# A fused neighbourhood-attention block on one core: VectorE's instruction list reordered within the band loop

## The reference

```python
h1 = n1_w * arcsinh(h) + n1_b
q, k, v = split(h1 @ qkv_w + qkv_b)            # 8 heads of 32
scores = q * hd**-0.5 . k[3 x 3 neighbourhood] # clipped at the image's edge
out = softmax(scores) @ v[3 x 3 neighbourhood]
h = h + out @ proj_w + proj_b
h2 = n2_w * arcsinh(h) + n2_b
return h + gelu(h2 @ mlp_w1 + mlp_b1) @ mlp_w2 + mlp_b2
```

## Time and profile before

| | |
|---|---|
| median of three runs | 4443.3 us |
| the profiled execution | 4440.94 us |
| its span, first to last instruction | 4439.1 us |
| mean granted TensorE clock | 0.992 of full speed |
| busy PE / DVE / ACT / POOL | 94% / 88% / 82% / 76% |

### The profile page before, as it was taken

The page is one execution under the profiler, slowest core; times in us unless marked ns, Lnnn a source line. Parts: engine busy times, 40 slices in busy tenths (PEclk is TensorE's granted clock), DMA queues, the critical chain, the costliest instruction groups (busy, mean ns, idle before and its releaser), DMA issues.

```text
span 4439.1 us, 129514 instructions
## 1 busy us (share of the span) xinstructions
PE 4159.5 (94%) x49224; PEld 2857.8 (64%) x49224; DVE 3926.1 (88%) x8225; ACT 3631.7 (82%) x5377; POOL 3359.0 (76%) x4092
## 2 busy tenths in 40 slices
PE   5999999999999999999999999999999999999997
PEld 3666666666666666666666666666666666666664
DVE  6899999989989998998999899899989989999984
ACT  4888888888888888888888888888888888888884
POOL 2777777777777777777777777777777777777775
PEclk8999999999999999999999999999999999999998
DMA  4555555555555555555555555555555555555551
GB/s 120 132 141 139 142 139 143 136 139 141 141 140 140 142 137 139 141 140 141 140 142 137 140 141 139 140 141 141 139 139 144 136 140 140 141 141 138 142 133 50
DMA packets 644105, 607.94 MB, mean 137 GB/s; under 512 B 77070, under 2 KB 639376, under 8 KB 639888
## 3 DMA queue, kind: packets, MB, share of 16 engines
q1 hardware_dynamic: 643488, 599.66, 51.2%
HBM read 206.02 MB, written 135.40 MB: 77 GB/s over the span
## 4 chain that ended last, share of the span: by engine, by line
DVE 42%; PE 18%; POOL 13%; issue 13%; ACT 12%; SPq 1%; DMA 0%; POOLq 0%; DVEq 0%; ACTq 0%
PE ps L381 16%; POOL b_lo L1163 6%; POOL b_hi L1161 6%; DVE ps L841 5%; DVE queries L860 5%; DVE o_norm L874 4%; DVE ln_u L767 4%; DVE ln_u L760 4%; DVE k_nat L815 4%; ACT L1073 4%; DVE ln_u L763 3%; DVE h L802 3%; ACT p_hi L1064 3%; DVE q_nat L808 3%; ACT prob L1063 2%
## 5 line engine op out<-in xcount | busy, mean ns | idle before, releaser
L1146 POOL TENSOR_TENSOR p_lo<-prob,p_hi 100x512 f16<-100x512 f32 x1024 | 1269.7, 1245 | 619.1 <-ACT p_hi L1064 619.1
L1063 ACT ACTIVATE prob<-ps 100x512 f32<-100x512 f32 x1024 | 610.2, 596 | 51.1 <-PE ps L381 49.3
L874 DVE TENSOR_TENSOR o_norm<-ps,recip 64x128 f32<-64x128 f32 x2048 | 590.2, 288 | 49.3
L1172 POOL TENSOR_TENSOR g_lo<-g,g_hi 128x512 f16<-128x512 f32 x512 | 593.8, 1160 | 41.0
L1064 ACT ACTIVATE p_hi<-ps 100x512 f16<-100x512 f32 x1024 | 616.4, 602 | 0.0
L381 PEld LDWEIGHTS ps<-v_win,p_hi 100*128 100x128 f16 x8192 | 476.0, 98 | 204.7 <-issue 66.9
L381 PE MATMUL ps<-w_hi,g_hi 128*128 128x256 f16 x2048 | 561.1, 274 | 0.0
L841 DVE TENSOR_REDUCE ps<-ps 128x8 f32<-128x800 f32 x512 | 509.1, 994 | 58.6 <-PE ps L381 54.2
L381 PE MATMUL ps<-w_lo,g_hi 128*128 128x256 f16 x2048 | 560.9, 274 | 0.0
L381 PE MATMUL ps<-w_hi,g_lo 128*128 128x256 f16 x2048 | 560.8, 274 | 0.0
L381 PE MATMUL ps<-v_win,p_hi 100*128 100x65 f16 x8192 | 515.6, 193 | 27.0 <-POOL p_lo L1146 18.4
(11 more groups left out here) (100 smaller groups left out, 11497.9 us busy)
## 6 DMA issues: line engine op xcount, KB each, us to landing
keys<-k_win SPq DMA_DIRECT2D x1536, 100.0 KB, 2.3
v_win<-v_rows SPq DMA_DIRECT2D x1024, 101.6 KB
queries<-q_nat SPq DMA_DIRECT2D x1536, 64.0 KB
v_rows<-v_nat SPq DMA_DIRECT2D x256, 260.0 KB, 4.3
xin<-in_x_dram SPq DMA_DIRECT2D x128, 512.0 KB, 4.3
out_dram<-y SPq DMA_DIRECT2D x256, 256.0 KB, 3.0
queries<-in_query_mask_dram SPq DMA_DIRECT2D x128, 224.0 KB
keys<-in_mlp_w_dram SPq DMA_DIRECT2D x2, 512.0 KB, 6.5
```

The costliest lines, as they stand in the source:

```text
L874: s = v.tensor_tensor(o_norm[r, c], av[r, :, HD * e:HD * e + HD], recip[c % 2][r].to_broadcast([NQ, PAIRS, HD]), ALU.mult)
L1063: act.activation(prob[b][0:NK], ps[0:NK, B_ST + b, :], ACT.Exp, scale=INV * INV).then_inc(prob_ready, 1)
L1146: pool.tensor_tensor(p_lo[b][0:NK], prob[b][0:NK], p_hi[b][0:NK], ALU.subtract).then_inc(p_lo_ready, 1)
L1172: pool.tensor_tensor(g_lo[:, m, :], g32[:, m, :], g_hi[:, m, :], ALU.subtract).then_inc(g_lo_ready, 1)
```

## The change

The change moves calls in two lists; no instruction is added or taken away. On DVE, within the slots:

- slot 0: `k_low` 1 goes in front of the copies `maxima_to_queries`;
- slot 1: `q_low` 1 and x's first evacuation go in front of the copies; x's second evacuation stays behind them;
- slot 2: `sign2` goes in front of `maximum`, and `sum1_` in front of the copies;
- slot 3: `sign1` and then `o_low` (first half) go in front of `maximum`.

On PE, in slot 3 only, `max_rows` goes from in front of `mlp_in` 2 to behind it, in front of `mlp_in` 3. In slots 0 to 2 it stays where it was.

```diff
                     if att:
                         weighted(t, par, 2 * k)
-                    if more:
+                    if k < 3 and more:
                         max_rows(ahead[0], ahead[2])
...
                     if k == 3 and post:
                         mlp_in(t - 1, 2)
+                    if k == 3 and more:
+                        max_rows(ahead[0], ahead[2])
+                    if k == 3 and post:
                         mlp_in(t - 1, 3)
...
                 for k in range(SLOTS):
                     ta, ka = (t, k + 1) if k + 1 < SLOTS else (t + 1, 0)
                     more = has(ta)
+                    if k == 2 and post:
+                        sign2(t - 1, old)
+                    if k == 3 and fill:
+                        sign1(t + 3, (u + 3) % XT)
+                    if k == 3 and att:
+                        o_low(t, par, 0)
                     if more:
                         maximum(ta, ka)
                         maximum_high(ta, ka)
...
                     if k == 1 and pre:
                         q_low(t + 2, par, 0)
-                    if k == 2 and post:
-                        sign2(t - 1, old)
-                    if k == 3 and att:
-                        o_low(t, par, 0)
-                    if k == 3 and fill:
-                        sign1(t + 3, (u + 3) % XT)
 
                     if att:
                         sum_reciprocal(t, 2 * k)
                         normalise(t, 2 * k)
-                    if more:
-                        maxima_to_queries(ta, par if ta == t else old, ka)
-
                     if k == 0 and pre:
                         k_low(t + 2, 1)
-                    if k == 0 and post:
-                        h_from_projection(t - 1, old, (u - 1) % XT, 0)
-                        h_from_projection(t - 1, old, (u - 1) % XT, 1)
                     if k == 1 and pre:
                         q_low(t + 2, par, 1)
                     if k == 1 and fill:
                         x_from_transposes(t + 3, (u + 3) % XT, 0)
+                    if k == 2 and fill:
+                        sum1_(t + 3)
+                    if more:
+                        maxima_to_queries(ta, par if ta == t else old, ka)
+
+                    if k == 0 and post:
+                        h_from_projection(t - 1, old, (u - 1) % XT, 0)
+                        h_from_projection(t - 1, old, (u - 1) % XT, 1)
+                    if k == 1 and fill:
                         x_from_transposes(t + 3, (u + 3) % XT, 1)
                     if k == 1 and post:
                         sum2_(t - 1)
                     if k == 1 and pre:
                         v_low(t + 2, 0)
-                    if k == 2 and fill:
-                        sum1_(t + 3)
```

## The result

The changed kernel takes 4914.53 us (median of 4 runs, 4911.74 to 4914.88) beside 4442.43 us before (4 runs, 4440.06 to 4443.96): a ratio of 1.1062, 95% interval 1.1043 to 1.1081. The direction was forecast, the size was not: 4757 us, with 4810 as the upper end. The profiled execution has a span of 4913.1 us, 474.0 more than before.

What follows compares the result with a forecast made beforehand. The bound was a loop from the fourth gelu through ACT, DVE and PE. Per band 0.68 (order) + 1.42 (port) + 0.4 (slot 3) made 2.5 us; 123 bands, 307 us, plus 7 at the ends, gave 4757 us, range 4700 to 4810.

Steps and rivals of the forecast that it cites:

- What bounds the kernel: A loop of one band, 33.73 us: fourth gelu, ACT to `k_high` 0, DVE's list, PE's list through `mlp_in` 3.
- Slot 1, the 0.15 and TensorE's regained wait: Slot 1: `q_low` 1 and PE's `x_transposes` 1 start 0.90 us earlier; the loop gains only DVE's vanished 0.15 us wait.
- Slot 2, 0.68 us a band: Slot 2: `sign2` before the maximum makes PE 1.15 us late at `max_rows`; less 0.47 slack, 0.68 us a band.
- Magnitudes wait for the port: DVE/POOL port: a magnitude arriving second waits for POOL's instruction; three meetings with `p_low` add 1.42 us a band.
- fewer meetings: Rival: a magnitude never waits, or `p_low` misses `magnitude2`; some 1.5 us a band, 4630 us; chance 0.26.
- The signs to look for: In the changed trace: PE idle 1.2 us or more at slot 2's `max_rows`, both magnitudes 1.3 to 1.5, `sign2` 1.8.
- `magnitude2`, the step that failed: Slot 0: `p_low` begins 0.2 us ahead of `magnitude2`, which ends at 2215.52 and not 2214.70: +0.82 us.
- DVE's sum is unchanged: Slot 0: putting `k_low` 1 before the copies costs DVE nothing; the copies come 0.66 us later, still ahead of `scores_t`.
- Slot 3, +0.4: Slot 3: DVE first on the port costs PE some 0.2 us; POOL first, some 0.55 late; 0.4 us taken.
- The clock: named as a rival: Part of the rival "more", over 4810 us: a lower granted TensorE clock behind longer idle spells; that rival's chance 0.06.

Runs made afterwards that it cites:

- e5: Slot 1's part of the change alone (`q_low` 1 and x's first evacuation before the copies), on the kernel before: 4415.55 us, ratio 0.9941.
- e7: `sign2` alone moved in front of slot 2's maximum, on the kernel before: 4522.86 us, ratio 1.0182.
- e2: The changed kernel with `sign2` alone put back behind the low part of slot 2's maxima: 4725.0 us, ratio 1.0645.
- the trials: Short port tests behind the end of the kernel before: a VectorE magnitude or sign arrives during a GpSimd instruction; magnitudes took 0.69 to 2.92 us.
- e3: The changed kernel with `magnitude2` moved before slot 0's second reciprocal and normalise, `k_low` 1 left early: 4667.35 us, ratio 1.0515.
- e1: The changed kernel with slot 0 put back, `k_low` 1 behind the copies again: 4648.97 us, ratio 1.0474.
- e9: Slot 3's part of the change alone, both the VectorE and TensorE lists, on the kernel before: 4510.15 us, ratio 1.0158.
- e10: The changed kernel with TensorE's `max_rows` of slot 2 moved behind `mlp_out` 1: 4858.73 us, ratio 1.0943.
- e6: The kernel before with the change's slot 1, and `magnitude1` moved before that slot's second reciprocal and normalise: 4366.14 us, ratio 0.983.
- e11: The changed kernel with slot 2's `max_rows` behind `mlp_out` 1 and both magnitudes before their slots' second reciprocal and normalise: 4568.26 us, ratio 1.0289.

## Why the prediction was right in direction and short in size

**What bounds the kernel: right.** The loop starts at the same wait after the change (118.0 us), and the stretch from the fourth gelu to `k_low` 0 has its 5.16 us unchanged.

**Slot 1, the 0.15 and TensorE's regained wait: right.** In a regular band `x_transposes` 1 starts at 2567.93, 0.06 behind `q_low` 1's end at 2567.87, with no idle time shown. e5 gives -0.21 us a band for this part with its meetings, where the same steps say -0.22.

**Slot 2, 0.68 us a band: right in kind and near in size.** e7 shows it alone: 1.21 us late at `max_rows`, 0.53 absorbed. The equal 0.68 is luck, as said there. e2 is no measure of it: the 1.44 us that come back hold `sign2`'s wait for the port too.

**Magnitudes wait for the port: right in kind.** It was the choice between bounds that no row settled. `magnitude1` +0.26 (predicted 0.33) and `sign2` +0.27 (predicted 0.27) are each a wait for one instruction. The rival "fewer meetings" is out. The signs to look for were put badly: "both magnitudes at 1.3 to 1.5 us" does not follow from the sum, which has `magnitude1` at 1.02, and neither came out there (2.43 and 0.95).

**`magnitude2`, the step that failed.** The prediction bounded a magnitude's wait by the rest of *one* GpSimd instruction, and took +0.82. It measured +1.74: the second `p_low` passed it. That is 0.92 us a band, 113 of the 157 us by which the forecast was short. The rows before showed VectorE only against one instruction or against pairs whose second was ready early, and the bound was drawn from them as if GpSimd's queue behind the running instruction could not count. By the Trainium skill (SBUF — State Buffer, section "SBUF: two separate sides") whoever starts first holds the pair of ports for the whole instruction. The traces agree for each single instruction: in the band read and in the trials a waiting magnitude ended 0.54 to 0.56 us behind the GpSimd instruction that held it last. Who gets the ports next when two wait is another question, and here it cost 0.92 us a band beside the 0.82 of the first wait. The same miss made a wait that the forecast did not have: TensorE stands 1.87 us at slot 1's `max_rows` in every band, since the maxima of that slot follow `magnitude2` in VectorE's list.

**The copies, a small miss.** "DVE's sum is unchanged" overlooked that the copies begin 0.13 us later behind `k_low` 1 than `h_from_projection` did. They stand in VectorE's list ahead of it, on the loop: 0.13 x 123 = 16 us. e3, which keeps this order, has a band 0.15 longer than e1, which does not.

**Slot 3, +0.4: right in sum, as a mean of two cases.** The second stretch of the loop had to lose 0.47 of slack and shows -0.02, so slot 3 cost 0.45. It was the case in which GpSimd is first, forecast at 0.55: `sign1` takes 2.19, and TensorE waits for `o_low` at `mlp_in` 2 (2585.77, 41.2 us in 124 waits over the run). The other case, VectorE first, had 0.2; alone, in e9, it costs 0.57.

**The clock: named as a rival, but given no price.** 33 us came from bands in which TensorE was granted 1.2 GHz for a few us. The falls go with the wait of 1.87 at slot 1, and so with the long `magnitude2`. They occur in the steady part of the three kernels that have both (the changed one, e2, e10) and in none of e1, e3, e5, e6, e7, e9 and e11. In e2 there is no wait at slot 2, and the clock falls all the same; e1 and e3 keep the wait of 1.75 at slot 2 alone, and it does not fall. In the changed kernel the same waits stand in every regular band, and the clock fell in 33 bands, 14 of them long ones. Why in these and not in the others stays open.

The three terms, 113 + 16 + 33 = 162 us, against a shortfall of 4914.5 - 4757 = 157. The differences of the other steps are small and partly cancel.

## What to carry to other kernels

In lists that are fixed by hand, moving an instruction ahead is paid by whatever it passes: ask for each of these which engine's list stops at it, as TensorE's did at `max_rows`, before counting what the moved one gains. An engine freed earlier shifts its whole tail: here a free 0.9 us on ScalarE moved a GpSimd instruction 0.6 us forward, to just in front of a VectorE instruction that shares its port, and undoing that one step (e1) gave back 266 us, 6% of the kernel, the falls of the clock with it. Where two engines share a port, order them so that the one on the loop starts first: in e6 moving `magnitude1` just ahead of its `p_low` took 1.1% off e5, and with e5's new order of slot 1 it is 1.7% off the kernel before. Look at which one the loop runs through, too: in e9 VectorE was first, and the loop ran through the `p_low` that paid.

## What the runs showed of the hardware

- A VectorE magnitude in SBUF (0.69 us alone) that comes during a GpSimd tensor_tensor of 1.16 us ends 0.54 to 0.56 us behind it; a sign with two SBUF inputs (1.21 alone) ends 1.08 behind it. If VectorE is first, the GpSimd instruction pays instead (1.63 and 2.16 us for 1.16).
- A VectorE instruction that waited for the port was passed by GpSimd's next one when that one's own semaphore wait ended during the first: 2.43 us in every full band of the changed kernel, 2.56 and 2.59 in the trials, 3.12 for a sign. When the next was ready from the start, VectorE got in between in all trials in which it arrived 0.2 to 0.4 us into the first (1.29 to 1.48 for a magnitude, 1.82 and 2.01 for a sign). One trial, 2.92 us, has no explanation here.
- TensorE's granted clock fell to 1.2 GHz behind idle spells of 1.9 us in three kernels, in some bands and not in others that look alike; in kernels whose longest regular idle spell was 1.75 us it did not fall in the steady part.
